# Splitting a normalised row into two 16-bit parts before the transpose instead of after it

## The reference, cut to what matters

```python
N, D = 2708, 512                       # x is N x D, adj is N x N of 0 and 1
h = jnp.maximum(_layernorm(x, axis=-1), 0.0)
x = x + _L0_gnn_ref(h, adj, L0_gnn_W, L0_gnn_a, L0_gnn_wtrans)    # attention, then @ wtrans (1024 x 512)
h = jnp.maximum(_layernorm(x, axis=-1), 0.0)
x = x + _L1_gnn_ref(h, adj, adj, ...)
h = jnp.maximum(_layernorm(x, axis=-1), 0.0)
x = x + _L2_gnn_ref(h, adj, L2_gnn_W)
h = jnp.maximum(_layernorm(x, axis=-1), 0.0)
x = x + _L3_gnn_ref(h, adj, L3_gnn_weight, L3_gnn_bias, L3_gnn_node_w, L3_gnn_edge_w)

def _layernorm(x, axis=-1, eps=1e-5):
    m = jnp.mean(x, axis=axis, keepdims=True)
    v = jnp.var(x, axis=axis, keepdims=True)
    return (x - m) / jnp.sqrt(v + eps)

# layer 3 begins with three products of the same h
node_att = jax.nn.softmax(h @ node_w, axis=0)
support, edges = h @ weight, h @ edge_w
```

## Time and profile before

| | us |
|---|---|
| median of 3 runs | 3085.52 (3084.68 to 3086.34) |
| the profiled execution, whole | 3081.91 |
| its span, first to last instruction | 3080.1 |
| PE busy | 2698.3 (88%) |
| DVE busy | 1982.6 (64%) |
| ACT busy | 1704.1 (55%) |
| POOL busy | 202.3 (7%) |
| PE busy from 40 to 160 us, in prep0 | 120.00 |

### The profile page before, as it was taken

The page is one execution under the profiler, slowest core; times in us unless marked ns, Lnnn a source line. Parts: engine busy times, 40 slices in busy tenths (PEclk is TensorE's granted clock), DMA queues, the critical chain, the costliest instruction groups (busy, mean ns, idle before and its releaser), DMA issues. The chain is left out here.

```text
span 3080.1 us, 57310 instructions
## 1 busy us (share of the span) xinstructions
PE 2698.3 (88%) x21599; PEld 1650.0 (54%) x21599; DVE 1982.6 (64%) x3600; ACT 1704.1 (55%) x2939; POOL 202.3 (7%) x103
## 2 busy tenths in 40 slices
PE   6929999999984599999999737499599999999999
PEld 4514444444442398888888613244266455555554
DVE  4639999999967688888888598422464333333332
ACT  2328888888863488888888537311133433232332
POOL 3710000000000000000000060000000000000000
PEclk9969999999996799999999868799799999999999
DMA  3033434434323441111111240132340212121210
GB/s 117 0 128 120 153 118 137 156 127 147 100 80 124 152 155 34 39 34 39 36 39 25 71 150 34 45 102 86 136 151 29 96 51 77 51 77 51 77 51 18
DMA packets 129394, 263.02 MB, mean 85 GB/s; under 512 B 58699, under 2 KB 61479, under 8 KB 122043
## 3 DMA queue, kind: packets, MB, share of 16 engines
q1 hardware_dynamic: 122875, 228.89, 22.0%
q10 hardware_dynamic: 6336, 31.72, 3.2%
HBM read 204.44 MB, written 56.14 MB: 85 GB/s over the span
## 5 line engine op out<-in xcount | busy, mean ns | idle before, releaser
L1373 PE MATMUL m_acc<-m_y,m_b 128*128 128x260 f16 x3872 | 661.3, 275 | 36.7 <-DVE m_b L1219 30.6
L1376 PE MATMUL m_acc<-m_y,m_at 128*128 128x130 f16 x3872 | 659.4, 221 | 0.0
L1188 ACT ACTIVATE m_above<-m_u,m_nvs 128x512 bf16<-128x512 f32 (+1 forms) x864 | 520.6, 682 | 80.7 <-DVE m_b L1219 79.7
L1373 PEld LDWEIGHTS m_acc<-m_y,m_b 128*128 128x128 f16 x3872 | 376.5, 97 | 99.8 <-issue 30.2
L804 PE MATMUL m_acc<-keep_z_hi,m_p_hi 128*128 128x512 f16 x968 | 365.5, 378 | 57.1 <-DVE m_p_lo L659 54.1
L1376 PEld LDWEIGHTS m_acc<-m_y,m_at 128*128 128x128 f16 x3872 | 381.1, 98 | 0.0
L805 PE MATMUL m_acc<-keep_z_lo,m_p_hi 128*128 128x512 f16 x968 | 366.0, 378 | 0.0
L808 PE MATMUL m_acc<-keep_z_hi,m_p_lo 128*128 128x512 f16 x968 | 365.0, 377 | 0.0
L1219 DVE TENSOR_TENSOR m_b<-m_above,m_at 128x1024 f16<-128x1024 bf16 (+1 forms) x432 | 279.1, 654 | 77.4 <-PE m_acc L1376 43.1
L2060 DVE CUSTOM_DVE_ANT_0 m_em<-m_sc,m_am 128x512 f32<-128x512 f32 x132 | 85.2, 647 | 326.0 <-PE m_sc L2004 313.4
L2134 ACT ACTIVATE m_wT_hi<-m_tw 128x1024 f16<-128x1024 f16 (+1 forms) x66 | 62.9, 953 | 396.4 <-PE m_tw L2017 396.4
(11 more groups left out here) (261 smaller groups left out, 5486.9 us busy)
## 6 DMA issues: line engine op xcount, KB each, us to landing
m_a_rows<-adj ACTq DMA_DIRECT2D x44, 704.0 KB, 4.3
m_at<-adjT SPq DMA_DIRECT2D x22, 1408.0 KB, 8.2
m_a<-adj SPq DMA_DIRECT2D x22, 1408.0 KB, 6.4
at<-m_at SPq DMA_DIRECT2D x22, 704.0 KB, 4.3
m_at<-at SPq DMA_DIRECT2D x22, 704.0 KB, 4.4
m_at<-at SPq DMA_DIRECT2D x5, 2816.0 KB, 17.7
p_x_all<-x SPq DMA_DIRECT2D x8, 1536.0 KB, 12.6
m_u<-rows SPq DMA_DIRECT2D x40, 256.0 KB, 3.7
```

The lines of the kernel that those rows point to most:

```text
L1188: act.activation(pair(above, a % RA, nb)[:, i], u[:, g % RU, 0:nb], ACT.Relu, bias=nvs[:, k, 2 * p + i:2 * p + i + 1], scale=STEEP).then_i ...
L1373: pe.matmul(full.rearrange("p l y e -> p (l y e)"), pair(b01, (m // 2) % RB, nb)[:, m % 2, q // 2, half], y12[:, k % 2, j].rearrange("p l ...
L1376: last = pe.matmul(full[:, :, 1, :], at[:, i0 + q // 2, j, half], y2[:, k % 2, j], start=False, stop=(j == T - 1), skip_group_check=True)
```

## The change

A tile is split before it is turned. `normalise` now issues two activations of the same input: `h` in 32 bits and `h_hi` in 16 bits, both in SBUF. `rest`, a new step on DVE with lead 3, takes `h_lo` = `h` - `h_hi`, from SBUF to SBUF. `transpose` turns both parts, eight 16-bit blocks in place of four 32-bit ones, into a 16-bit PSUM tile of the same size in bytes. `high` copies both at once (128 x 1024, 16 bits to 16 bits) into the one tile `hT`. `split` is gone from DVE. The ring semaphore `lo_done` is replaced by `hi_ready`. In prep0 the short transpose of `uv` at the end writes into `main` and so waits for the last `low` also. `prep3` gets the same edits, but for this last.

```diff
--- before.py
+++ after.py
@@ prep0
-        hT_hi, hT_lo = kit.sb("hT_hi", [2, KC, P], F16), kit.sb("hT_lo", [2, KC, P], F16)
+        h_hi, h_lo = kit.sb("h_hi", [2, D], F16), kit.sb("h_lo", [2, D], F16)
+        hT = kit.sb("hT", [2, 2, KC, P], F16)
...
-        tp = kit.ps("tp", [2, KC, P])
+        tp = kit.ps("tp", [2, 2, KC, P], F16)
...
+        tail = main[:, 1, 0:P]
...
-                for ring in (lo_done, prod_done, z_lo_done, uv_done):
+                for ring in (hi_ready, prod_done, z_lo_done, uv_done):
...
                     act.activation(h[:, b, :], flat(x_all[:, ds(t, 1), :]), ACT.Relu,
+                                   bias=nmr[:, b:b + 1], scale=rstd[:, b:b + 1])
+                    act.activation(h_hi[:, b, :], flat(x_all[:, ds(t, 1), :]), ACT.Relu,
                                    bias=nmr[:, b:b + 1], scale=rstd[:, b:b + 1]).then_inc(h_ready, 1)
...
                     act.wait_ge(tp_ready, done(t))
                     act.wait_ge(prod_done, free(t))
-                    act.activation(hT_hi[:, b], tp[:, b], ACT.Copy).then_inc(hi_ready, 1)
+                    act.activation(hT[:, b], tp[:, b], ACT.Copy).then_inc(hi_ready, 1)
...
                 def transpose(t, b):
-                    pe.wait_ge(h_ready, t + 1)
-                    pe.wait_ge(lo_done, free(t))
-                    for k in range(KC):
-                        last = pe.transpose(tp[:, b, k, :], h[:, b, k * P:(k + 1) * P], keep["ident"][:])
+                    pe.wait_ge(rest_made, t + 1)
+                    pe.wait_ge(hi_ready, free(t))
+                    for i, part in enumerate((h_hi, h_lo)):
+                        for k in range(KC):
+                            last = pe.transpose(tp[:, b, i, k, :], part[:, b, k * P:(k + 1) * P], keep["ident16"][:])
                     last.then_inc(tp_ready, 1)
 
                 def products(t, b):
-                    pe.wait_ge(hi_ready, t + 1)
-                    pe.wait_ge(lo_done, done(t))
+                    pe.wait_ge(hi_ready, done(t))
                     pe.wait_ge(z_lo_done, free(t))
...
-                        split_product(pe, main[:, b, cols], hT_hi[:, b], hT_lo[:, b], w_hi, w_lo, cols)
+                        split_product(pe, main[:, b, cols], hT[:, b, 0], hT[:, b, 1], w_hi, w_lo, cols)
...
                 pe.wait_ge(uv_done, done(T - 1))
-                pe.transpose(tp[0:2 * T, 0, 0, :], uv[:].rearrange("p s t -> p (s t)"), keep["ident"][:]).then_inc(uvt_ready, 1)
+                pe.wait_ge(z_lo_done, done(T - 1))
+                pe.transpose(tail[0:2 * T, :], uv[:].rearrange("p s t -> p (s t)"), keep["ident"][:]).then_inc(uvt_ready, 1)
...
-                def split(t, b):
-                    dve.wait_ge(hi_ready, t + 1)
-                    dve.tensor_tensor(hT_lo[:, b], tp[:, b], hT_hi[:, b], ALU.subtract).then_inc(lo_done, 1)
+                def rest(t, b):
+                    dve.wait_ge(h_ready, t + 1)
+                    dve.wait_ge(tp_ready, free(t))
+                    dve.tensor_tensor(h_lo[:, b, :], h[:, b, :], h_hi[:, b, :], ALU.subtract).then_inc(rest_made, 1)
...
-                pipeline(dve, (0, dots), (2, split), (5, lambda t, b: moments(dve, t, b, x_all, stats, mv, std, s, gate)),
-                         (4, lambda t, b: shift(dve, t, b, mv, std, rstd, nmr, h_ready, s, gate)), (0, low),
+                pipeline(dve, (0, dots), (5, lambda t, b: moments(dve, t, b, x_all, stats, mv, std, s, gate)),
+                         (4, lambda t, b: shift(dve, t, b, mv, std, rstd, nmr, h_ready, s, gate)),
+                         (3, rest), (0, low),
...
```

More of the change, by code:

```diff
@@ L359, in products @@
                         cols = slice(half * D, (half + 1) * D)
-                        split_product(pe, main[:, b, cols], hT_hi[:, b], hT_lo[:, b], w_hi, w_lo, cols)
+                        split_product(pe, main[:, b, cols], hT[:, b, 0], hT[:, b, 1], w_hi, w_lo, cols)
                     pe.wait_ge(uv_done, done(t - 1))
-                    last = split_product(pe, small[:, b, 0:2], hT_hi[:, b], hT_lo[:, b], w_hi, w_lo, slice(2 * D, NX))
+                    last = split_product(pe, small[:, b, 0:2], hT[:, b, 0], hT[:, b, 1], w_hi, w_lo, slice(2 * D, NX))
                     last.then_inc(prod_done, 1)
@@ L1794, in _ @@
             def _(sp):
-                for ring in (lo_done, prod_done, s_lo_done, e_lo_done, nl_done):
+                for ring in (hi_ready, prod_done, s_lo_done, e_lo_done, nl_done):
                     sp.sem_inc(ring, 2)
@@ L1843, in transpose @@
                 def transpose(t, b):
-                    pe.wait_ge(h_ready, t + 1)
-                    pe.wait_ge(lo_done, free(t))
-                    for k in range(KC):
-                        last = pe.transpose(tp[:, b, k, :], h[:, b, k * P:(k + 1) * P], keep["ident"][:])
+                    pe.wait_ge(rest_made, t + 1)
+                    pe.wait_ge(hi_ready, free(t))
+                    for i, part in enumerate((h_hi, h_lo)):
+                        for k in range(KC):
+                            last = pe.transpose(tp[:, b, i, k, :], part[:, b, k * P:(k + 1) * P], keep["ident16"][:])
                     last.then_inc(tp_ready, 1)
                 def products(t, b):
-                    pe.wait_ge(lo_done, done(t))
+                    pe.wait_ge(hi_ready, done(t))
                     pe.wait_ge(s_lo_done, free(t))
-                    split_product(pe, main[:, b, :], hT_hi[:, b], hT_lo[:, b], w_hi, w_lo, slice(0, D))
+                    split_product(pe, main[:, b, :], hT[:, b, 0], hT[:, b, 1], w_hi, w_lo, slice(0, D))
                     pe.wait_ge(e_lo_done, free(t))
@@ L1857, in products @@
                         for k in range(KC):
-                            for n, (a, b_) in enumerate(((w_hi, hT_hi), (w_lo, hT_hi), (w_hi, hT_lo))):
-                                pe.matmul(edge[:, b, m, :], a[:, k, of], b_[:, b, k, :], start=(m == 0 and k == 0 and n == 0),
+                            for n, (a, i) in enumerate(((w_hi, 0), (w_lo, 0), (w_hi, 1))):
+                                pe.matmul(edge[:, b, m, :], a[:, k, of], hT[:, b, i, k, :], start=(m == 0 and k == 0 and n == 0),
                                           stop=(k == KC - 1 and n == 2), skip_group_check=True)
                     pe.wait_ge(nl_done, done(t - 1))
-                    split_product(pe, small[:, b, 0:1], hT_hi[:, b], hT_lo[:, b], w_hi, w_lo, slice(2 * D, NX)).then_inc(prod_done, 1)
+                    split_product(pe, small[:, b, 0:1], hT[:, b, 0], hT[:, b, 1], w_hi, w_lo, slice(2 * D, NX)).then_inc(prod_done, 1)
                 pipeline(pe, (2, transpose), (1, products),
```

12 lines of the change are left out of this document (6 added, 6 removed).

## The result

The changed kernel takes 3092.59 us (median of 20 runs, 3088.86 to 3099.79); the kernel before, on the same chip, 3086.22 (20 runs, 3083.91 to 3090.8). The ratio is 1.0021, with a 95% interval from 1.0014 to 1.0028: 6.4 us slower, between 4.3 and 8.6. A second comparison of the same two programs gave 1.0027 [1.0018, 1.0036]. Forecast were 3094.3 us, +8.8, and a range of 3089.5 to 3103.

What follows compares the result with a forecast made beforehand. PE was taken to bound the loops, with POOL's additions delaying DVE in prep0, and a chain of single instructions each start. 3.6 + 2.0 + 3.8 - 0.6 = +8.8 us on 3085.5 gives 3094.3, range 3089.5 to 3103.

Steps and rivals of the forecast that it cites:

- Start of prep0: First product of prep0 comes 3.6 us late, through a chain of subtractions, longer `high` and extra activation that nothing hides.
- Loop of prep0: From step 0's turns to the last products, 127.05 us in place of 125.05: +2.0, with POOL holding the subtraction.
- Rounds of three steps: In prep0's loop, subtraction and POOL's pair meet in a cycle of 5.93 + 5.93 + 6.42 = 18.28 us.
- the 0.55 us behind POOL: In prep0's loop, a held subtraction ends 0.55 us after POOL's addition does.
- POOL's 0.24: Gap between POOL's two additions in prep0's loop; a waiting subtraction takes it and holds POOL up.
- the rival without a hold: POOL doesn't hold the subtraction, so prep0's loop gains 0.9 us: +5.9 in all, 3091.4; chance 15%.
- that of POOL always winning: POOL always wins the gap: prep0's steps take 6.63 us, +12 over 18 steps, +19 in all, 3104; chance 12%.
- Start of prep3: Same chain as in prep0, but with a later `nmr`(1): first product of prep3 3.8 us late.
- Loop of prep3: PE's turns cost 0.03 us less per tile, -0.6 over 20 steps; steps with a `residual` chunk hold the same DVE work.
- The `uv` turn at nothing: At prep0's end the turn waits for the last `low`, but POOL's later end gives 4.9 us of cover: no cost.
- Turns nearly free on PE: Rival: turns slip in between PE's products, up to 0.47 us per tile gained; at 0.4, 3078 us; chance 4%.
- the cheap start: Rival: PE reaches 2.4 GHz at the same moment, late products gain up to 1.8 us per stage: +5.2, 3090.7; 13%.

Runs made afterwards that it cites:

- bare loops: Prep0 loops of the changed kernel and the kernel before, each with POOL's additions left out: 112.67 and 113.20 us; whole times 3084.06 and 3080.73 us.
- second pair: The changed kernel and the kernel before, both run again word for word: ratio 1.0027 [1.0018, 1.0036].
- kernels with one half: The change in prep0 alone or in prep3 alone, the other as before: 3089.06 and 3088.86 against 3086.41 us, each 1.0011.
- ACT's order: Changed kernel with `root` and `normalise` ahead of `high` on ACT in both preparations: 3084.88 against 3086.41 us for the kernel before, 0.9997.

## Why the prediction was right, and where not

- **Start of prep0, forecast +3.6.** Measured +3.44 (8.02 - 4.58), by the chain of the forecast.
- **Loop of prep0, forecast +2.0.** The last product starts at 169.04, 126.70 us after the turns of step 0; before it was 164.53 - 39.46 = 125.07. So it costs +1.63; 126.70 stands against the forecast 127.05. Rounds of three steps, both orders of meeting, the 0.55 us behind POOL and POOL's 0.24 are all in the rows. The 0.35 less lies in the first and the shorter rounds (6.20, 6.32, 6.31 in place of 6.42). That the hold is the cause is shown twice, by `h` in PSUM and by the additions left out; the rival without a hold (-0.9) and that of POOL always winning (+12) both fall. A third idea, that only ACT's longer chain costs the loop, falls too, since both kernels keep that chain. The order in ACT's list counts all the same: with `normalise` ahead of `high` the subtraction is no longer held and the loop is 112.67 too.
- **Start of prep3, forecast +3.8.** Measured +3.43. The extra 0.2 was for an `nmr`(1) that comes 2.16 us after `nmr`(0) (2238.00 - 2235.84), not 1.93 as in prep0. In this profile of the changed kernel it came after 1.94 (2243.50 - 2241.56), so there was nothing extra; with prep3 alone changed it came after 2.16, and the start was 8.24, +3.65. With prep0 alone changed it comes after 1.95 in the untouched prep3, so this goes with the code of prep0 as well.
- **Loop of prep3, forecast -0.6.** This is the step that failed: measured +0.3. It held that the steps with a chunk "hold the same amount of DVE's work as before". They do, but the turns now wait for an instruction at the end of it, which costs 0.11 by itself; and it took prep3's steps to depend on prep3's code alone, which they don't: the new prep0 adds 0.35 behind that chunk. Together that is +0.46 in two steps in place of -0.06. The other 17 steps take 6.043 on average, against 6.051: a third of the -0.03 came. Many are 6.02, as forecast, every second late one is 6.08. With prep3 alone changed all 17 are 6.02 or 6.03, so the -0.03 per tile comes whole there, and the loop is 0.35 shorter than before. The trace has no wait of PE at the 6.08, and what makes them stays open.
- **The `uv` turn at nothing.** It came late by its wait, and POOL still ends the stage: 7.4 us from the last product to the end of POOL's last addition, before (171.92 - 164.53) and after (174.31 + 2.12 - 169.04).
- **Turns nearly free on PE: falls.** All 19 steps of the bare loops are 5.93 against 5.96.
- **Sum, forecast +8.8.** From the first `nmr` to the last turns, the preparations are 5.09 and 4.02 us longer, together 9.1 of the 9.9 between the two spans; the rest lies in stages that don't differ in code. In the second pair they are 6.4 and 3.7 longer, 10.1 with 9.7 between the spans; 1.25 of it is the longer stretch from the first product to step 0, where 11 products of prep0 run at the lower clock in place of 5. By the forecast's own terms the profiles give 3.44 + 1.63 + 3.43 + 0.32 = 8.8, just the sum that was forecast. That exact hit is luck: three terms were 0.2 to 0.4 too high and one 0.9 too low.
- **Slips in the working.** `high` starts 0.73 behind the turns by the rows used (87.87 - 87.14), not 0.70. The 0.89 in the earlier trace rows is how long DVE had been idle before `low`, which `z_hi` ended, not a time since the products; their end at 164.9 is right all the same (164.53 + 0.38). That `low` isn't held by POOL was read from an overlap of 0.07 us; the changed kernel shows it fully. And the low end of the range, 3089.5, is called the cheap start, whose own sum is 3090.7. None of this changes the forecast.

The medians say less than the profiles: +6.4 [4.3, 8.6] and +7.6 (its ratio's interval makes it 5.6 to 11.1). The medians of the halves sum to 5.1, with 2.8 us of uncertainty on each. Whether the undisturbed cost is nearer 6.4 or 9 isn't settled. The profiles show one thing that blurs whole times: the second attention and the preparation behind it take either some 767 + 118 us or some 760.5 + 127.6, 3 us apart in sum, in kernels whose code there is the same. Both profiles of the kernel before and both of the changed one show the first, so it doesn't touch their difference. The kernels with one half, with `h` in PSUM and with ACT's order show the second, so their whole times may be off by these 3 us. Whether it changes from run to run or goes with the program isn't shown; the expectation that a second profile of the kernel before would differ there was not borne out.

## What to carry to other kernels

When an instruction of VectorE moves its operand from PSUM to SBUF, look who else reads SBUF at that time: here the subtractions that met POOL's additions cost 2.6 us, and nothing once one operand was back in PSUM. A step added to a loop with slack is paid at each stage's start, where the pipeline is one chain (3.4 us twice here); the order in a queue decides over half of it, and reordering one engine's queue gave 1.9 of each 3.4 back. Count not only how much work a queue holds in a step, but what stands behind it: when a consumer's input moves to the end of a queue, a burst ahead of it can become a stall (0.1 us here). And before a small difference in one stage is put down to an edit there, change that stage alone: here an edit in the first preparation moved a step of the fourth by 0.35 us.

## What the runs showed of the hardware

- A held VectorE instruction isn't stretched by a fixed sum: it ends 0.01 to 0.03 us (128 x 1) or 0.54 to 0.56 us (128 x 512) after POOL's. Both are some 0.14 less than it lasts when free (0.16 and 0.69), so nearly all of its work seems to come afterwards. The 128 x 512 one lasts up to 2.51 us in the changed kernel.
- The hold goes both ways. The 0.24 us between two dependent additions of POOL are enough for a waiting subtraction to go first, and POOL's addition then lasts 2.37 instead of 2.13 (2.29 to 2.47 in all six cases of the changed kernel).
- Eight 16-bit turns of 128 x 128 in the loop take 0.44 us of PE's list in prep0 too (85.09 - 84.65), 0.055 each, four 32-bit ones 0.12 each.
- An activation with a 128 x 1024 result in 16 bits from PSUM takes 1.02 us, in both preparations as in the last stage.
